# An attention kernel of 32 images: the first image's projections moved up by two or three slots, with narrower waits, and an earlier load of the third image

## The reference, cut to what matters

```python
x = x + gate_layer(group_norm(x))     # a gate per channel, from pooled means and a sampled 3-tap convolution
x = x + attention(group_norm(x))      # below
# attention, per image:
q = relu_bn(w2q @ relu_bn(w1q @ x));  k = relu_bn(w2k @ relu_bn(w1k @ x));  v = wv @ x + bv
sim = softmax over 27 taps (3x3 windows, dilations 1, 2 and 4) of  k(shifted) . q
out = wo @ sum(sim * v(shifted)) + bo
```

## Time and profile before

| | |
|---|---|
| median of 3 runs | 1530.93 us (1530.9 to 1531.99) |
| the profiled execution | 1530.86 us |
| its span, first to last instruction | 1529.1 us |
| PE busy in the span | 1467.3 us, 96% |
| DVE, ACT, POOL busy | 1241.0 us (81%), 1167.7 us (76%), 776.9 us (51%) |
| chain that ended last, by engine | PE 80%, DVE 6%, issue 4%, ACT 4%, POOL 3%, DMA 2% |

### The profile page before, as it was taken

How to read it: one execution, slowest core, us unless ns; L and a number is a source line. 1 busy time by engine, 2 the same in 40 slices (tenths; PEclk the granted TensorE clock), 3 DMA queues, 4 the chain that set the end, 5 groups by cost and what they waited for, 6 DMA issues and landing times.

```text
span 1529.1 us, 35557 instructions
## 1 busy us (share of the span) xinstructions
PE 1467.3 (96%) x9287; PEld 1198.9 (78%) x9287; DVE 1241.0 (81%) x4629; ACT 1167.7 (76%) x3044; POOL 776.9 (51%) x2185
## 2 busy tenths in 40 slices
PE   2899999999999999999999999999999999999997
PEld 1687887888887888888788888888888888877886
DVE  7588888888888888888888888888888888888775
ACT  2577778777777778777778777778777777787776
POOL 6545455545465545465545455545455554455530
PEclk9999999999999999999999999999999999999999
DMA  2335443445444445443445444445544455543344
GB/s 91 92 104 165 150 140 104 134 148 165 149 125 115 136 149 165 150 127 110 141 150 161 153 123 113 141 150 157 157 123 111 138 155 155 158 122 109 97 116 140
DMA packets 104709, 205.99 MB, mean 135 GB/s; under 512 B 13632, under 2 KB 83776, under 8 KB 96448
## 3 DMA queue, kind: packets, MB, share of 16 engines
q1 hardware_dynamic: 103632, 203.49, 44.9%
q10 hardware_dynamic: 880, 0.23, 0.1%
HBM read 51.62 MB, written 51.38 MB: 67 GB/s over the span
## 4 chain that ended last, share of the span: by engine, by line
PE 80%; DVE 6%; issue 4%; ACT 4%; POOL 3%; DMA 2%; SPq 0%; ACTq 0%; DVEq 0%; POOLq 0%
PE ps_s L421 19%; PE ps_o L454 16%; PE ps_v L494 10%; PE ps_t L433 9%; PE ps_p L471 9%; PE ps_p L476 9%; PE ps_o L459 3%; DVE e L971 2%; DVE e L954 2%; ACT qq L624 1%; ACT eT L607 1%; ACT e L592 1%; DMA raw<-in_x_dram 1%; POOL g L767 1%; PE ps_v L510 1%
## 5 line engine op out<-in xcount | busy, mean ns | idle before, releaser
L592 ACT ACTIVATE e<-e,zmin 128x256 f32<-128x256 f32 x800 | 403.6, 504 | 184.7 <-DVE zmin L954 176.7
L454 PEld LDWEIGHTS ps_o<-eT,v 128*128 128x128 f32 x2688 | 380.3, 191 | 85.4 <-issue 81.5
L454 PE MATMUL ps_o<-eT,v 128*128 128x128 f32 x2688 | 433.5, 276 | 0.3 <-ACT eT L607 0.3
L954 DVE CUSTOM_DVE_ANT_0 e<-ps_s,mask 128x256 f32<-128x256 f32 x800 | 337.8, 422 | 111.1 <-PE ps_s L421 106.2
L421 PE MATMUL ps_s<-kk,qq 128*128 128x256 f32 x1408 | 428.0, 386 | 0.0
L433 PE MATMUL ps_t<-ident,e 128*128 128x128 f32 x1600 | 305.9, 273 | 0.2 <-DVE e L971 0.2
L433 PEld LDWEIGHTS ps_t<-ident,e 128*128 128x128 f32 x1600 | 225.1, 141 | 81.0 <-DVE e L971 0.5
L607 ACT ACTIVATE eT<-ps_t 128x512 f32<-128x512 f32 (+1 forms) x416 | 235.6, 566 | 69.2 <-PE ps_t L433 67.4
L971 DVE SCALAR_TENSOR_TENSOR e<-e,rz,keep 128x256 f32<-128x256 f32 x480 | 262.0, 546 | 0.1
L421 PEld LDWEIGHTS ps_s<-kk,qq 128*128 128x128 f32 x1408 | 224.0, 192 | 47.2 <-issue 41.1
L494 PE MATMUL ps_v<-wvox,xb 128*128 128x128 f32 x1600 | 220.0, 278 | 0.8 <-DVE v L992 0.8
(11 more groups left out here) (147 smaller groups left out, 1818.8 us busy)
## 6 DMA issues: line engine op xcount, KB each, us to landing
out_dram<-raw SPq DMA_DIRECT2D x32, 1568.0 KB, 5.7
raw<-in_x_dram SPq DMA_DIRECT2D x31, 1568.0 KB, 6.5
v<-v SPq DMA_DIRECT2D x192, 224.0 KB, 2.9
kk<-kk SPq DMA_DIRECT2D x192, 112.0 KB, 2.2
ksp<-kk SPq DMA_DIRECT2D x192, 64.0 KB, 2.1
v<-v_last SPq DMA_DIRECT2D x64, 128.0 KB, 2.9
kk<-kk SPq DMA_DIRECT2D x32, 224.0 KB, 2.9
v<-v_last SPq DMA_DIRECT2D x64, 96.0 KB, 2.7
```

Source lines behind the costliest of these rows:

```text
L454: last = nc.tensor.matmul(o[:, UPIX * (u - 1):UPIX * (u + 1)], v[:, s, u, :], eT[:, UPIX * (base + 2 * u - 1):UPIX * (base + 2 * u + 1)], ...
L592: nc.scalar.activation(e[:, i, :], e[:, i, :], ACT.Exp, bias=zmin[:, i:i + 1], scale=-1.0, accum_out=zs[:, i:i + 1]).then_inc(e_done.next( ...
L954: nc.vector.tensor_tensor_reduce(e[:, i, :], ps_s[(TILES * n.parity() + t) % 2][:, 0:KEYS], mask[:].rearrange("p s h a b -> p (s h a b)"), ...
```

## The change

Three edits. Image 0's projections of strips 0, 1 and 2 are issued 3, 3 and 2 slots sooner, on PE, ACT and SP alike, with the relu, the second matmul, the key and query writes and the key copies. Strip 0's first matmul waits for `w1x` alone (step 35 of `pg`), the wait for the bias `b1x` (step 17 of `dg`) stands on ACT ahead of the relu, and the wait for `wvox` (step 36) stands on PE ahead of the first value matmul; these three waits are changed for every image. Image 2 is loaded at slot 0 of image -1 rather than at slot 19.

```diff
+EARLY = (3, 3, 2)
+
+def g_slots(m):
+    return [at - (EARLY[g] if m.offset == 0 and g < len(EARLY) else 0) for g, at in enumerate(G_SLOT)]
...
-                        if t == LOAD and (n + 3).exists():
+                        if t == (LOAD if n.offset != -1 else 0) and (n + 3).exists():
                             load(n + 3)
                         for m, rel in items_at(n, t):
-                            for g, at in enumerate(G_SLOT):
+                            for g, at in enumerate(g_slots(m)):
                                 if rel == at + 2:
                                     keys(m, g)
...
                     def hidden(m, g):
                         if g == 0:
-                            pe.wait_ge(dg.sem, dg.count(m, 17))
-                            pe.wait_ge(pg.sem, pg.count(m, 36))
+                            pe.wait_ge(pg.sem, pg.count(m, 35))
...
+                        if b == 0:
+                            pe.wait_ge(pg.sem, pg.count(m, 36))
                         held = [k for k, at in CHAIN_READS if CH[at] <= V_SLOT[b]]
...
-                            for g, at in enumerate(G_SLOT):
+                            for g, at in enumerate(g_slots(m)):
                                 if rel == at:
                                     hidden(m, g)
...
-                            for g, at in enumerate(G_SLOT):
+                            for g, at in enumerate(g_slots(m)):
                                 if rel == at + 1:
                                     query_and_key(m, g)
...
                         act.wait_ge(h_ps.sem, h_ps.count(m, g + 1))
+                        if g == 0:
+                            act.wait_ge(dg.sem, dg.count(m, 17))
...
                             for g in RELU_FIRST:
-                                if rel == G_SLOT[g]:
+                                if rel == g_slots(m)[g]:
                                     hidden(m, g)
...
-                            for g, at in enumerate(G_SLOT):
+                            for g, at in enumerate(g_slots(m)):
                                 if rel == at and g not in RELU_FIRST:
```

## The result

The changed kernel takes 1534.62 us, the median of 14 runs (1532.79 to 1536.88); the kernel before took 1532.02 us beside it (14 runs, 1529.79 to 1533.23). The ratio is 1.0019, 95% interval 1.0012 to 1.0026: 2.9 us slower, 1.8 to 4.0. The forecast was 1530.3, at most 1532.8. It stood on 1530.93 for the kernel before, which measured 1.1 us more in this comparison; that alone did not put the time above the range, which allowed for a loss of 1.9 us where the change cost 2.9. The profiled execution after took 1532.79, the fastest of its 14, with a span of 1531.1.

The account below looks back on a forecast made before the run. From about 60 us PE's own work was taken to bound the kernel, so the worth lay in the head: -1.0 (a4) + 0.4 (low stretch) = -0.6 us, from 1530.9 to 1530.3 us; range 1528.2 to 1532.8, 8 in 10.

Parts of the forecast that it names:

- a4 behind r2: On ACT in the head: r2 stands between strip 1's writes and a4, which starts at 49.0 or 50.0, against 50.02.
- the -1.0 of a4 in the sum: Head: a4, and c4 with it, comes 1.0 us sooner, taking the clock's early rise.
- early rise of the clock: PE's clock in the head rises at 44.9, after the last halt, instead of about 47; a4 then starts at about 49.0.
- PE's halt ahead of c4: PE's halt ahead of k3 grows from 1.04 to about 2.5 us, that ahead of c4 stays 1.96; low stretch costs 0.4.
- The price of 1.7 us for the low stretch: Behind c4 PE runs 3.4 us at the low clock, which costs half its length, 1.7 us.
- c1's delay: Head: c1 starts 3.15 us later, covered if c3 comes after 44.8; as a rival, not covered, 1533.5 us, chance 4%.
- c3 waited for v1's add in the open: Head: c3 follows v1 at once and waits 0.6 us for its add, which PE no longer hides.
- The load: Image 2's sooner load on SP makes nothing late on DVE; cost taken as 0.
- three signs of being wrong: c4 not following a4 at 9.9 us, PE waiting for something new behind 60 us, or c4 before 57.5.
- The halts cost more than the order gains: Rival on PE's clock: no sooner rise, a4 at 50.0 to 50.9, low stretch up to doubled; 1532.2 us, chance 20%.
- some 0.9 late: Head: if the clock were low all through, a4 would start some 0.9 us late.
- slower by over 0.2%: Whole kernel: time over 1534.0 us, the tail of the halts' and c1's cases; chance 4%.

Follow-up runs that it names:

- second profile: The kernel before run once more, unchanged: 1529.24 us in its one run.
- the load back: The changed kernel with image 2's load back at slot 19: 1.0018 to the kernel before.
- the filled kernels: The changed kernel and the kernel before, each with idle matmuls in PE's halts ahead of k3 and c4: 1.0010 and 0.9992 to the kernel before.
- the head filled as well: The kernel with a4 first, halts filled and strip 0's residual base later, plus idle matmuls ahead of the first projections: 0.9964 to the kernel before, 1525.67 us.

## Why the prediction was wrong

**The step that failed** is "a4 behind r2". It put a4 at the end of slot 20, behind strip 2's relu alone. The table `CH` has a4 at 21 (slot 21 of image -1, for image 1). In the old order slot 21 holds no key or query writes, strip 1's being in slot 20, so the error was without consequence there. After the change strip 2's second matmul and its writes are in slot 21, and on ACT writes stand ahead of chain steps. With the forecast's own durations the right place gives: c3's end at 47.5 or 48.5, r2's end at 49.0 or 50.0, k2 1.0 more, the writes 1.58 more, so a4 at 51.6 or 52.6 instead of 49.0 or 50.0. Measured were 51.20 and 52.48. That alone would have forecast 1.6 to 2.6 us slower.

**A second step that failed** is the gain itself, the -1.0 of a4 in the sum. It sets an early rise of the clock after the change (a4 at 49.0) against the late one of the only profile before (50.02). The second profile has a4 at 48.26 with an early rise. Early against early and late against late, the change moves a4 from 48.26 to 51.20 and from 50.02 to 52.48: 2.9 and 2.5 us. With these few profiles the pairing is a reading, not a proof. The medians moved by 2.9 (1.8 to 4.0). Nor is the gain there with a4 in the place that the forecast gave it: with a late rise it starts at 49.39 instead of 50.02, with an early one it could start no sooner than the positions allow, 48.58, against 48.26, and that kernel measured 1.0003. c3 now stands behind v0, k1 and v1, and with an early rise it comes at 46.60 where it came at 44.80. That the change brings the rise forward is not shown either: k1 took 0.92 in one profile with the new head and 1.15 to 1.70 in six others, while h1 took 0.92 in two of the four with the old one.

**"PE's halt ahead of c4" followed from the same error.** I had strip 2's writes behind a4, and PE done 4.4 us after a4's start. They were ahead of it, and PE was done at 52.67, 1.5 us after; it then stood for 5.46 us ahead of k3, where I had 2.5. The clock did fall sooner in that halt: 0.82 in the us from 57 and 0.50 from 58 on, where the kernel before has 0.86 in the us from 60. By the rule of the Trainium skill ("TensorE: Matmul & The Clock Gate", "HAM oscillation — how this bites in real kernels") idle gaps bring the low rate back, and these rows agree that they did. Yet most of the loss is not this. Behind c4, where it counts, the low stretch was 3.4 us in this profile, as before, and 5.1 in the one with the load back, for 0.85 us; and the filled kernels differ by 0.0018, as the unfilled do by 0.0019 (each ratio within 0.0009). The price of 1.7 us for the low stretch of the kernel before was too high as well: in the profile with its halts filled, c4 of image 2 follows c4 of image 1 only 1.0 us sooner.

**What held.** h0 started at 34.72 (35.0 forecast) and k0 ended at 39.00 (39.28). c1's delay was covered: the diagonal ended at 43.46 (44.8 at the latest). PE worked from h1 on without a long halt, and in that execution the clock had risen by k1, which took 0.92. c3 waited for v1's add in the open, 0.65 us, and ran from 46.60 to 47.09, a little sooner than forecast (47.4 at the soonest). The positions came at 48.58 (49.0). c4 followed a4 by 9.9 us in all profiles with POOL's old order. The load cost nothing, nor did the waits as far as can be told. Of the three signs of being wrong that the forecast named none came; each looked at c4 or behind it, and none at the order ahead of a4.

**The rivals.** "The halts cost more than the order gains" had the right sign, and its condition was met (a low stretch of 6.8 us, a4 at 51.20), but the mechanism was another: it put the price on the clock and on c3's open wait, and a4 at 50.9 at the latest. None of the rivals had strip 2's writes ahead of a4. The bound of a4, "some 0.9 late", held only what stood before r2, and so the range ended 1.8 us below the measured time. The chance of slower by over 0.2%, 4%, was too small for the same reason; the measured 0.19% lies at that edge.

## What to carry to other kernels

When a hand-written order is shifted, write out the new order of every engine that the shift touches, not only of the one that is the bound: the loss here was, in the main, one group on ACT that came to stand behind three instructions with a wait of their own. Ask of each chain step what is ahead of it in its new slot. And look at two profiles before a difference of 2 us is explained from one: here the kernel before moved by 1.75 us between its own two.

## What the runs showed of the hardware

The TensorE clock in the head is not shown by the clock column, which reads 1.00 while the pair at L471 takes 1.84 us at 36.55 and 1.02 at 50.04 in the same profile; only the durations show it. When it rises differs from one execution to the next: in the two profiles of the unchanged kernel h1 at 44 to 45 us took 0.92 in one and 1.70 in the other, and c4 moved by 1.75 us with it. The chip of the first of these is not on record; but on the second chip three kernels with the same order up to k1 had k1 at 1.15, 1.70 and 1.55, so the chip is not all of it. What sets the moment of the rise these runs leave open. Keeping PE busy with idle matmuls removed the low stretch behind c4 in every kernel that had them; for three of them there is the same kernel without, and the gain was 0.0008 to 0.0010 each, with intervals of 0.0009 on either side. With the head filled as well the kernel came to 0.9964, which was more than any reordering of the first projections gave.
